# A vision tower on one core: in the third attention block, the second half's query and key products and their statistics placed ahead of the first half's column sums

## The reference

```python
h = h + _L1_attn_ref(_layernorm(h), ...)                 # layer C

def _L1_attn_ref(x, Wq, Wk, bk, Wv, bv, gq, gk, Wo, bo):  # 12 heads of 16
    q = layernorm_nobias(x @ Wq.T, gq)
    k = layernorm_nobias(x @ Wk.T + bk, gk)
    v = x @ Wv.T + bv
    scores = jnp.einsum('bnqd,bnkd->bnqk', q, k) * scale
    attn = jax.nn.softmax(scores, axis=-2)               # over the queries: a column softmax
    o = jnp.einsum('bnqk,bnkd->bnqd', attn, v)
    return o @ Wo.T + bo + x
```

## Time and profile before

| what | value |
|---|---|
| time, median of 3 runs | 507.44 us (499.46, 507.44, 508.05) |
| the profiled execution's own time | 501.84 us |
| its span, first to last instruction | 500.1 us |
| mean granted clock of PE | 0.971 |
| busy: PE, PE weight loads, DVE, ACT, POOL | 460.0, 396.2, 260.1, 174.7, 88.9 us |
| share of the chain that ended last | PE 80%, DVE 11%, ACT 3%, issue 3%, DMA 2% |

### The profile page before, as it was taken

How to read it: one execution, slowest core, us unless ns; L and a number is a source line. 1 busy time by engine, 2 the same in 40 slices (tenths; PEclk the granted TensorE clock), 3 DMA queues, 4 the chain that set the end, 5 groups by cost and what they waited for, 6 DMA issues and landing times.

```text
span 500.1 us, 9635 instructions
## 1 busy us (share of the span) xinstructions
PE 460.0 (92%) x3788; PEld 396.2 (79%) x3788; DVE 260.1 (52%) x714; ACT 174.7 (35%) x427; POOL 88.9 (18%) x154
## 2 busy tenths in 40 slices
PE   4799999989999998999999998899999999999990
PEld 4766776878887887887765878788998989999990
DVE  4287744654658476563553546786567632212212
ACT  0332243133341462726273441375312103343340
POOL 2022100002121202002200002420012137722211
PEclk9999989999999999999999999999999589999996
DMA  8950000000030000000000720015621002898603
GB/s 302 239 129 1 1 2 0 1 2 1 1 93 1 1 1 2 2 1 1 0 1 0 225 62 1 1 55 157 223 77 35 6 26 61 277 295 274 202 2 109
DMA packets 14820, 35.93 MB, mean 72 GB/s; under 512 B 2719, under 2 KB 8223, under 8 KB 14582
## 3 DMA queue, kind: packets, MB, share of 16 engines
q1 hardware_dynamic: 12424, 31.42, 20.9%
q0 software_dynamic: 1632, 2.59, 1.7%
q10 hardware_dynamic: 720, 1.32, 0.7%
HBM read 32.49 MB, written 3.59 MB: 72 GB/s over the span
## 4 chain that ended last, share of the span: by engine, by line
PE 80%; DVE 11%; ACT 3%; issue 3%; DMA 2%; POOL 0%; SPq 0%; POOLq 0%; DVEq 0%; ACTq 0%
PE bank L1435 11%; PE bank L1382 9%; PE bank L1473 7%; PE bank L1415 6%; PE bank L1657 6%; PE bank L1459 5%; PE bank L1749 4%; PE bank L1703 4%; PE bank L1718 3%; PE bank L1463 3%; PE bank L1690 3%; PE bank L1488 3%; PE bank L1424 2%; PE bank L1673 2%; PE bank L1396 1%
## 5 line engine op out<-in xcount | busy, mean ns | idle before, releaser
L574 POOL TENSOR_TENSOR rstd<-rstd_tmp,minus_half 111x3 f32<-111x3 f32 x20 | 17.2, 858 | 294.0 <-DVE rstd_tmp L899 294.0
L1382 PE MATMUL bank<-constants 128*128 128x128 f32 x514 | 67.4, 288 | 0.0
L1382 PEld LDWEIGHTS bank<-constants 128*128 128x128 f32 x514 | 63.8, 201 | 2.3 <-issue 1.4
L1435 PE MATMUL bank<-arena 96*111 96x192 f32 (+1 forms) x320 | 56.8, 327 | 0.0
L1435 PEld LDWEIGHTS bank<-arena 96*111 96x111 f32 (+1 forms) x320 | 52.1, 175 | 2.2 <-issue 2.1
L1415 PE MATMUL bank<-nT,arena 96*96 96x296 f32 (+1 forms) x144 | 39.7, 420 | 0.8 <-DVE nT L914 0.8
L1473 PE MATMUL bank<-arena,et 128*128 128x192 f32 x204 | 37.4, 334 | 0.0
L704 ACT ACTIVATE xn<-h,minus_mean_rstd,rstd 111x192 f32<-111x192 f32 (+1 forms) x48 | 22.6, 536 | 37.9 <-POOL minus_mean_rstd L581 37.9
L936 DVE TENSOR_TENSOR vblk<-bank,constants 111x384 f32<-111x384 f32 x40 | 21.8, 555 | 26.1 <-PE bank L1435 17.9
L1473 PEld LDWEIGHTS bank<-arena,et 128*128 128x128 f32 x204 | 32.7, 190 | 1.9
L1657 PE MATMUL bank<-arena,qT 96*64 96x222 f32 (+1 forms) x320 | 32.4, 354 | 1.0 <-DVE arena L927 0.7
(11 more groups left out here) (263 smaller groups left out, 782.0 us busy)
## 6 DMA issues: line engine op xcount, KB each, us to landing
arena<-in_w SPq DMA_DIRECT2D x17, 576.0 KB, 5.6
arena<-in_w SPq DMA_DIRECT2D x17, 384.0 KB, 3.7
arena<-in_w SPq DMA_DIRECT2D x34, 96.0 KB, 4.1
arena<-in_patches SPq DMA_DIRECT2D x4, 606.0 KB, 7.8
arena<-in_c SPq DMA_DIRECT2D x2, 576.0 KB, 10.5
arena<-in_wpack SPq DMA_DIRECT2D x2, 576.0 KB
arena<-in_wpack SPq DMA_DIRECT2D x1, 1152.0 KB
arena<-in_wpack SPq DMA_DIRECT2D x1, 1008.0 KB
```

Of the source, the lines that this page charges most:

```text
L1382: mm(PS[b][:, 0:128], ident, ident, start=True, stop=True)
L1435: last = mm(o, nrep[q][k][0:96 + k, im], w(n + "_qkv", k, 2 * D, D), start=(k == 0), stop=(k == 1 and n != "B"))
```

## The change

Two neighbouring digits of `ORDER` are exchanged (entries 43 and 44, counted from 0): K of half 1 now stands ahead of N of half 0. The number of fillers ahead of O of layer C, half 0, goes from 12 to 22, and the number ahead of R becomes one for each half: 19 as before for half 0, 2 for half 1.

```diff
-IDLE_R = 19
-IDLE_O = {("B", 0): 12, ("C", 0): 12, ("C", 1): 15, ("G", 1): 14}
+IDLE_R = (19, 2)
+IDLE_O = {("B", 0): 12, ("C", 0): 22, ("C", 1): 15, ("G", 1): 14}
...
-ORDER = ("0010100010101101101010110010000101010101010010100110110111001010011011010101011001001010100110110110101001010100110110010111")
+ORDER = ("0010100010101101101010110010000101010101010100100110110111001010011011010101011001001010100110110110101001010100110110010111")
...
-                    keep_busy(("k", n, q, 0), IDLE_R)
+                    keep_busy(("k", n, q, 0), IDLE_R[q])
```

## The result

The changed kernel took 506.03 us in the median of six runs (504.45 to 507.82), beside 503.59 us for the kernel before in its six (498.88 to 508.05). The ratio is 1.0101, with an interval of 1.0061 to 1.0141: 1% slower, where 0.4% faster was forecast.

A forecast was written before the change was run, and what follows sets the result against it. PE, busy 460.0 of 500.1 us, was taken as the bound, waiting behind fillers in layer C for DVE and POOL. The 1.83 us gain off the profiled 501.84 gave 500.0 us, range 497.0 to 507.4.

The forecast's parts named there:

- The bound of the stretch: Layer C, half 1: column sums, statistics, POOL, norming and the fillers ahead of R set the end, 0.3 us apart.
- the change on DVE and PE: Layer C: norming ends 1.97 us earlier, O starts 2.13 us later, R's transposes start 1.83 us earlier.
- The lock between POOL and DVE: Rival, 10%: L964 stalls beside POOL's power, at most 1.21 us; gain 0.62 us, time 501.2. The forecast took nothing.
- the one on a path not shortened: Rival, 8%: something else taken as covered releases R, such as late products or O's copies on ACT; time 501.8.
- I take the whole 1.83 us as carried to the end: From layer C to the kernel's end: the full gain carries through, 501.84 to 500.0 us.
- the list 497.6, 505.6, 506.2: Forecast times in us of the three timed runs, made by taking 1.83 off each.
- The rival on the clock: Rival, 12%: with seven fillers gone PE's clock falls, seen between 158 and 180 us, costing up to 8.5 us; time 508.5.
- The spread of the timed runs: Whole kernel: runs from 499.46 to 508.05, 8.6 us, far larger than the effect, so the range follows it.

The follow-up runs named there:

- e1: Changed kernel with the fillers of before (12 ahead of O, 19 ahead of R), so the new order alone: mean 508.1 us.
- f1: Changed kernel run a third time with no edit: mean 501.3 us, ratio 0.9976 to the kernel before.
- e8: Changed kernel with 16 fillers in place of 8 ahead of the transposes of layer D, half 1: mean 503.0 us.
- e5: Changed kernel with 33 fillers in place of 25 ahead of the transposes of layer F, half 1: mean 501.4 us.
- f4: Repeat of e5, the changed kernel with 33 fillers in place of 25 ahead of layer F, half 1: median 499.99 us, ratio 0.9969.
- e9: Changed kernel with 41 fillers in place of 25 ahead of the transposes of layer F, half 1: mean 502.2 us.
- e7: Kernel before, in its old order, with 33 fillers in place of 25 ahead of the transposes of layer F, half 1: mean 502.2 us.

## Why the prediction was wrong

- **The bound of the stretch, and the change on DVE and PE:** right. Statistics, POOL and norming came as worked out, the stretch is 1.82 us shorter where 1.83 was said, in every trace of the changed kernel that I measured (16.68 us each time). R with the old fillers would have lost 2.1 us; e1 lost 1.98.
- **The lock between POOL and DVE:** right to take nothing. All four L964 took 0.47 us, the first beside the power. The rule of the Trainium skill, "SBUF — State Buffer", section "Who interferes with whom", would have made that row 1.2 us longer (164.26 to 165.49); for the power the trace does not bear it out. That rival is dead, and so is the one on a path not shortened. L652, whose row I set against the power's, is a subtraction and not the multiplication that I called it; the argument does not hang on that.
- **"I take the whole 1.83 us as carried to the end":** this is the step that failed, together with the list 497.6, 505.6, 506.2 that I made by taking 1.83 off each run. It holds for the work, as the products show, but it supposes that the loss to the clock stays what it was. The term was missing from the sum: with all later stages moved by about 2 us, either way, the loss was some 3 us larger in the mean (17.7 at -1.8; 18.3, 18.3 and 20.0 at +2; 14.8 unmoved). In the traces the clock then falls in layer F, where it did not, and that makes up 2.5 us. The size is less sure than the place: in the last group the changed kernel's loss was 15.6.
- **The rival on the clock** had the right cause and the wrong place and size. I looked for the fall at 158 to 180 us, where fillers were taken out, and set 8.5 us on it. No trace of the changed kernel falls there; the price is about 3 us in the mean, and the fall that goes with it comes 150 us later. I gave it 12%.
- **The spread of the timed runs** was read rightly as larger than the effect, and the range held the median; but I put down nothing for a shift of that spread by the change itself, only for its width. That the median fell inside so wide a range says little for the mechanism. The median that I began from, 507.44 us of three runs, was itself high by chance: the 128 executions of that kernel beside the experiments have 501.9 in the median.

The Trainium skill, "TensorE: Matmul & The Clock Gate", section "What's actually happening", says that the window by which activity is judged runs free of the kernel's start. The traces agree with it: up to 125 us all kernels are the same program, and yet at 24 to 50 us the clock is 1.00 in nine executions and 0.74 to 0.87 in nine others. The counts by place (none of four, eight of nine) do not follow from that sentence. What stays open is why the place shows in means over many executions at all, if each begins anywhere in that rhythm, and why f1 went otherwise than the two groups before it. One possible cause was only argued: in the first 16 us PE's products run at either level, so a later rise of the clock also delays the program (the first 48 of them took 9.27 us in the changed kernel's trace, 7.88 in that of before), which would keep the two in part together.

## What to carry to other kernels

Give the gain of a shorter path and the loss to PE's clock as two terms: span times mean clock showed 1.7 us with an error of 0.15, where times alone, spread over 10 us, could not. Where an early stage is made 2 us shorter, look through all later stages for those in which PE waits, since the clock may now fall in one where it did not. Refilling the time elsewhere (e8) tests whether the place is the cause, and products added ahead of the stage that falls (e5, f4, e9) can lower the loss. Here the new order with eight more fillers ahead of layer F was ahead of the kernel before in two groups, 501.4 against 502.5 us and 499.7 against 501.5 (error of each difference 0.9), but each ratio's interval, 0.9927 to 1.0004 and 0.9936 to 1.0001, just reaches 1. The old order with the same eight fillers (e7) had 502.2 against 503.4, with an interval of 0.9876 to 0.9976, so how much of this is the new order is not shown.

## What the runs showed of the hardware that was not expected

In layer F, DVE is slowed beside POOL after all, as by a lock. DVE's two conversions to `n_quant` (L1266) read one SBUF tensor each and took 1.22 us in the changed kernel, while POOL added to `h` from 327.53 to 331.29:

```profile
329.63 1.22 DVE L1266 TENSOR_SCALAR n_quant<-arena 96x296 bf16<-96x296 f32 x2
```

```profile
327.53 3.76 POOL L602 TENSOR_TENSOR h<-h,parameters 111x384 f32<-111x384 f32 x4 [1.60 <-ACT xn L704]
```

In e5 the fillers delayed PE's transposes, POOL was done with all four of its additions at 327.67, and the conversions took 0.53 us:

```profile
327.87 0.53 DVE L1266 TENSOR_SCALAR n_quant<-arena 96x296 bf16<-96x296 f32 x2
```

That is 0.69 us, and it is most of the reason why fillers that took 1.79 us longer (7.53 us against 5.74) moved what follows by 1 us only. Beside POOL's power, by contrast, L964 (0.47 us) and, in the kernel before, L1059 (0.42 us) kept their time.
